# Scaled float16 halves for queries, outputs, experts and router, and shifts and norms moved to GpSimd, in a gated cross-attention and expert layer

## The reference, cut to what matters

```
x = x + tanh(g_xattn) * (softmax(LN(x) Wq (ctx Wk)^T / 8) (ctx Wv) Wo + bo)   # 16 heads of 64
x = x + tanh(g_ffn)   * sum over the 2 best of 8 experts of p_e (LN(x) We^T + be)
```

## Time and profile before

| | |
|---|---|
| runs | 1012.39, 1012.43, 1013.25 us |
| span of the profiled execution | 1009.9 us (its own total time isn't given apart from the runs; the span is 2.5 us below their median) |
| busy PE, DVE, ACT, POOL | 979.5, 821.2, 797.1, 622.4 us |
| chain that ended last | PE 79%, DVE 6%, issue 5%, ACT 4%, POOL 3% |
| DMA engines, transposes and all | 84.7% of 16 engines' span |
| granted clock of PE | full in all slices of the page but the first (0.9) |

### The profile page before, as it was taken

How to read it: one execution, slowest core, us unless ns; L and a number is a source line. 1 busy time by engine, 2 the same in 40 slices (tenths; PEclk the granted TensorE clock), 3 DMA queues, 4 the chain that set the end, 5 groups by cost and what they waited for, 6 DMA issues and landing times.

```text
span 1009.9 us, 27181 instructions
## 1 busy us (share of the span) xinstructions
PE 979.5 (97%) x10656; PEld 770.1 (76%) x10656; DVE 821.2 (81%) x1518; ACT 797.1 (79%) x1404; POOL 622.4 (62%) x371
## 2 busy tenths in 40 slices
PE   7798899999999999999999999999999999999998
PEld 5476777887777877778777787778777787777786
DVE  6577788888888878887888978888788887888768
ACT  5999999777997689886897779977799768987510
POOL 5897777555666557655675746755566655765500
PEclk9899999999999999999999999999999999999999
DMA  4999999787998699995998869977799868998610
GB/s 145 195 205 187 160 182 185 140 128 128 195 166 147 112 161 179 169 151 99 180 169 158 141 115 187 177 138 130 130 190 170 146 110 160 161 154 153 117 35 21
DMA packets 550062, 150.86 MB, mean 149 GB/s; under 512 B 537752, under 2 KB 547376, under 8 KB 549936
## 3 DMA queue, kind: packets, MB, share of 16 engines
q1 hardware_dynamic: 549936, 149.13, 84.7%
HBM read 11.70 MB, written 4.19 MB: 16 GB/s over the span
## 4 chain that ended last, share of the span: by engine, by line
PE 79%; DVE 6%; issue 5%; ACT 4%; POOL 3%; DMA 2%; SPq 0%; ACTq 0%; POOLq 0%; DVEq 0%
PE MB L1076 37%; PE ST L1212 17%; PE PV L1234 16%; PE MB L1088 4%; DVE nmax L873 3%; ACT pf L708 2%; DMA pt_s<-p_s 2%; POOL p_s L552 2%; PE ST L1076 1%; DVE acc L836 1%; PE ST L1243 1%; ACT p_s L718 1%; PE MB L1161 1%; DVE v_s L865 1%; POOL ex_s L590 1%
## 5 line engine op out<-in xcount | busy, mean ns | idle before, releaser
L552 POOL TENSOR_TENSOR p_s<-pf,p_s 128x1024 f16<-128x1024 f32 x254 | 544.3, 2148 | 312.6 <-ACT p_s L718 267.8
L873 DVE TENSOR_REDUCE nmax<-ST 128x2 f32<-128x1024 f32 x256 | 308.4, 1218 | 45.9 <-PE ST L1212 43.0
L708 ACT ACTIVATE pf<-ST,shifts 128x512 f32<-128x512 f32 x512 | 323.8, 688 | 7.6 <-POOL p_s L552 3.7
L718 ACT ACTIVATE p_s<-pf 128x1024 f16<-128x1024 f32 x254 | 267.7, 1060 | 4.2 <-DMA pt_s<-p_s 1.4
L1234 PEld LDWEIGHTS PV<-v_s,pt_s 128*128 128x128 f16 x6096 | 202.2, 98 | 76.7 <-issue 70.4
L1234 PE MATMUL PV<-v_s,pt_s 128*128 128x65 f16 x6096 | 228.8, 194 | 6.4 <-DMA pt_s<-p_s 5.2
L1076 PE MATMUL MB<-ex_s,x2t_s 128*128 128x512 f32 x708 | 189.0, 403 | 0.0
L1076 PEld LDWEIGHTS MB<-ex_s,x2t_s 128*128 128x128 f32 x708 | 126.8, 188 | 24.9
L699 ACT ACTIVATE shifts<-nmax 128x2 f32<-128x2 f32 x256 | 52.8, 206 | 115.8 <-DVE nmax L873 115.3
L836 DVE SCALAR_TENSOR_TENSOR acc<-MB,m,acc 128x256 f32<-128x256 f32 x236 | 113.9, 483 | 29.6 <-PE MB L1076 22.6
L1212 PE MATMUL ST<-KH,QH 64*128 64x512 f32 x512 | 123.0, 476 | 11.4 <-ACT pf L708 8.5
(11 more groups left out here) (141 smaller groups left out, 1047.4 us busy)
## 6 DMA issues: line engine op xcount, KB each, us to landing
pt_s<-p_s SPq DMA_TRANSPOSE x508, 3.4
xin<-x SPq DMA_DIRECT2D x7, 512.0 KB, 4.4
out<-acc SPq DMA_DIRECT2D x7, 512.0 KB, 3.7
kvin<-kv_t SPq DMA_DIRECT2D x8, 256.0 KB, 3.8
acc<-expert_t SPq DMA_DIRECT2D x6, 256.0 KB, 3.5
pf<-wq SPq DMA_DIRECT2D x1, 768.0 KB, 7.2
xin<-x SPq DMA_DIRECT2D x2, 256.0 KB, 2.8
pt_s<-wk SPq DMA_DIRECT2D x1, 512.0 KB, 5.8
```

What stands on the lines that cost most here:

```text
L552: pool.tensor_tensor(p_s[:, slot, 1, :, :], pf[:, u % 2, :, :], p_s[:, slot, 0, :, :], ALU.subtract).then_inc(p_lo, 1)
L708: last = act.activation(pf[:, u % 2, i, :], ST[u % 2][:, i, :], ACT.Exp, bias=shifts[:, u % 2, i:i + 1], scale=SCALE)
L718: act.activation(p_s[:, it.ring(p, u, P_SLOTS), 0, :, :], pf[:, u % 2, :, :], ACT.Copy).then_inc(p_hi, 1)
L873: dve.tensor_reduce(nmax[:, t % 2, :], ST[t % 2][:, :, :], AX.X, ALU.max, negate=True)\
```

## The change

Queries (wq_s, xt_s), output projection (wo_s, ot_s), experts (ex_s, x2t_s) and router (gt_s) are held as float16 high and low parts instead of fp32r; the matmuls on keys, values and scores stay as they are. So that float16 holds them, the weights are divided by a scale taken from their largest absolute value (a maximum over each partition on DVE, summed over the partitions by a small matmul, then five small DVE instructions), and the activations are scaled by 1024 in the norm. The scales go back in where the results are read out. For wq this is done in the prologue (`query_scale`), for the late weights in rows 2 to 8 of the first batch (`late_maximum`, `late_scales`, `gate_parts`); POOL multiplies each late block by its scale in rows 7 to 18, ahead of ACT's copy and POOL's subtraction, which before were in rows 3 to 17. The score scale 1/8 now lies in the query, so that the shift is an addition alone.

The shifts and the applied norms go from ACT to POOL. In POOL's table each row begins with the shift of unit n and goes on with the low part of unit n - 1 instead of n.

```diff
+W_RANGE = 2.0 ** 14
+X_SCALE = 2.0 ** 10
...
 POOL_ORDER = (
-    "low", "low", "low", "low", "low", "low", "low", "low power2", "low", "low residual", "low", "low", "low hold1",
-    "low hold2", "low hold3", "low", "low", "low", "low", "low", "low", "low", "low", "low context power1", "low",
-    "low", "low", "low", "low", "low", "low", "low",
+    "shift low", "shift low", "shift low", "shift low", "shift low", "shift low", "shift low", "shift low",
+    "shift low", "shift power2 norm2 low", "shift low residual", "shift low", "shift low", "shift low",
+    "shift hold1 low", "shift hold2 low", "shift hold3 low", "shift low", "shift low", "shift low", "shift low",
+    "shift low", "shift low", "shift low", "shift low", "shift low power1 norm1", "shift low context", "shift low",
+    "shift low", "shift low", "shift low", "shift low",
 )
 
-VALUES_BACK, SHIFT_BACK, EXP_BACK, COPY_BACK = 6, 0, 0, 0
+VALUES_BACK, LOW_BACK, EXP_BACK, COPY_BACK = 6, 1, 0, 0
...
-NEXT_JOBS = [("xt", 0), ("xt", 1), ("q", 0), ("k", 0), ("bound",), ("q", 1), ("k", 1)]
+NEXT_JOBS = [("xt", 0), ("xt", 1), ("q", 0), ("bound",), ("k", 0), ("q", 1), ("k", 1)]
...
-        wq_s = sb("wq_s", [P, 2, LC, INNER], F32R)
+        wq_s = sb("wq_s", [P, 2, LC, INNER], F16)
         wk_s = sb("wk_s", [P, 2, INNER], F32R)
         wv_s = sb("wv_s", [P, 2, INNER], F32R)
-        wo_s = sb("wo_s", [P, 2, PAIRS, DIM], F32R)
-        ex_s = sb("ex_s", [P, 2, LC, EXPERTS * DIM], F32R)
-        gt_s = sb("gt_s", [P, LC, 2, EXPERTS], F32R)
+        wo_s = sb("wo_s", [P, 2, PAIRS, DIM], F16)
+        ex_s = sb("ex_s", [P, 2, LC, EXPERTS * DIM], F16)
+        gt_s = sb("gt_s", [P, LC, 2, EXPERTS], F16)
...
+                if it.kind == FIRST and n == 0:
+                    sp.dma_start(stage_o[:, :, :], wo.rearrange("(c p) n -> p c n", p=P)).then_inc(wo_in, 16)
+                    sp.dma_start(stage_e[:, :, :], expert_t.rearrange("(c p) n -> p c n", p=P)).then_inc(ex_in, 16)
...
+            def normed(src, n, shift_done, done):
+
+                pool.wait_ge(shift_done, n)
+                for t in range(TT):
+                    last = pool.tensor_scalar(xn[:, t, :], src[:, t, :], rstd[:, t:t + 1], shift[:, t:t + 1],
+                                              ALU.mult, ALU.add)
+                last.then_inc(done, 1)
+
+            def first_norm(it):
+                pool.wait_ge(job_free, it.start(JOBS) + BANKS if it.kind == FIRST else
+                             it.done(JOBS, ("logits",)) + BANKS)
+                normed(xin, it.b + 2, ln1_shift, ln1_done)
+
+            def second_norm(it):
+                pool.wait_ge(job_free, it.start(JOBS) + BANKS)
+                normed(acc, it.b, ln2_shift, ln2_done)
+
+            def shift_of(b, p, u):
+
+                pool.wait_ge(max_done, unit_count(b, p, u))
+                pool.tensor_scalar(shifts[:, u % 2, :], nmax[:, u % 2, :], 1.0, P_SHIFT,
+                                   ALU.mult, ALU.add).then_inc(shift_ready, 1)
...
+                if it.kind == FIRST and 0 <= n - LATE_AT < LATE:
+                    h = n - LATE_AT
+                    if h == 0:
+                        pool.wait_ge(late_scale, 1)
+                    raw, of = late[h][0], late[h][3]
+                    pool.tensor_scalar(raw, raw, late_mul[:, of:of + 1], 1.0, ALU.mult, ALU.mult)\
+                        .then_inc(late_scaled, 1)
+                if it.kind == FIRST and 0 <= n - LATE_AT - LATE_LO < LATE:
+                    h = n - LATE_AT - LATE_LO
                     pool.wait_ge(late_hi, h + 1)
-                    pool.tensor_tensor(late[h][2], late_raw(h), late[h][1].bitcast(F32), ALU.subtract)\
-                        .then_inc(late_lo, 1)
-
-            run(row)
+                    pool.tensor_tensor(late[h][2], late[h][0], late[h][1], ALU.subtract).then_inc(late_lo, 1)
...
+                    act.wait_ge(wq_scale, 3)
+                    act.activation(wq_s[:, 0, :, early], stage_q[:, :, early], ACT.Copy, scale=q_mul[:, 0:1])\
+                       .then_inc(w_hi, 1)
+                    act.wait_ge(wv_in, 16)
+                    act.activation(wv_s[:, 0, :], stage_v, ACT.Copy).then_inc(w_hi, 1)
...
-            def shift_of(b, p, u):
-
-                act.wait_ge(max_done, unit_count(b, p, u))
-                act.activation(shifts[:, u % 2, :], nmax[:, u % 2, :], ACT.Identity, bias=P_SHIFT, scale=SCALE)\
-                   .then_inc(shift_ready, 1)
...
-                                          bias=shifts[:, u % 2, i:i + 1], scale=SCALE)
+                                          bias=shifts[:, u % 2, i:i + 1], scale=1.0)
...
-            def normed(src, n, shift_done, done):
-
-                act.wait_ge(shift_done, n)
-                for t in range(TT):
-                    last = act.activation(xn[:, t, :], src[:, t, :], ACT.Identity, bias=shift[:, t:t + 1],
-                                          scale=rstd[:, t:t + 1])
-                last.then_inc(done, 1)
...
+            def query_scale():
+
+                for n, (cols, landed) in enumerate(((early, wq_in), (rest, wq_rest_in))):
+                    dve.wait_ge(landed, 16)
+                    last = dve.tensor_reduce(wq_max[:, n:n + 1], stage_q[:, :, cols], AX.XY, ALU.max,
+                                             apply_absolute_value=True)
+                last.then_inc(wq_largest, 1)
+                dve.wait_ge(wq_summed, 1)
+                dve.tensor_reduce(q_back[:, :], sums_q, AX.X, ALU.max).then_inc(wq_scale, 1)
+                dve.wait_ge(wq_scale, 1)
+                dve.tensor_scalar(q_div[:, :], q_back[:, :], 1.0 / W_RANGE, 1e-30, ALU.mult, ALU.max)\
+                   .then_inc(wq_scale, 1)
+                dve.wait_ge(wq_scale, 2)
+                dve.tensor_scalar(q_back[:, :], q_div[:, :], SCALE / X_SCALE, None, ALU.mult)
+                dve.reciprocal(q_mul[:, :], q_div[:, :]).then_inc(wq_scale, 1)
...
+                if name == ("bound",):
+                    dve.wait_ge(wv_in, 16)
+                    dve.tensor_reduce(wv_max[:, :], stage_v, AX.X, ALU.max, apply_absolute_value=True)
+                    bound(0)
...
+            def rest_of_queries():
+                dve.wait_ge(w_hi, 4)
+                dve.scalar_tensor_tensor(wq_s[:, 1, :, rest], stage_q[:, :, rest], q_mul[:, 0:1],
+                                         wq_s[:, 0, :, rest], ALU.mult, ALU.subtract).then_inc(wq_rest_lo, 1)
...
+                if kind == FIRST and n == 1:
+                    rest_of_queries()
                 if kind == FIRST and n == 2:
                     constants()
+                if kind == FIRST and 0 <= n - LATE_MAX < 3:
+                    late_maximum(n - LATE_MAX)
+                if kind == FIRST and n == LATE_SUM:
+                    late_scales()
+                if kind == FIRST and n == LATE_AT + 1:
+                    gate_parts()
...
+                    pe.wait_ge(wq_largest, 1)
+                    summed(sums_q, wq_max[:, :], wq_summed)
```

More of the change, by code:

```diff
@@ L818, in take @@
                 elif kind == "router":
-                    last = dve.tensor_copy(logit_parts, m[0:2 * EXPERTS, :])
+                    last = dve.tensor_scalar(logit_parts, m[0:2 * EXPERTS, :], g_back[0:2 * EXPERTS, 0:1], None, ALU.mult)
                 elif kind == "gates":
@@ L1237, in values, with summed @@
                 last.then_inc(pv_ready, 1)
+            def summed(dst, largest, done):
+                pe.matmul(dst, ones[:, :].broadcast_to([P, P]), largest, start=True, stop=True).then_inc(done, 1)
             def keep_busy(n):
```

304 lines of the change are left out of this document (171 added, 133 removed).

## The result

The changed kernel takes 1070.18 us (median of four runs, 1068.18 to 1075.41) against 1012.41 for the kernel before on the same chip: a ratio of 1.058 (95% interval 1.0551 to 1.0608). I had forecast 1031, with a range of 1004 to 1048. It is slower, as forecast, but by 58 us and not by 19. The profiled execution took 1068.53 us, its span is 1066.7.

The account below looks back on a forecast made before the run. PE was taken to pace the middle batches, POOL, ACT and the transposes the first. 1009.9 + 26.3 + 10 + 17 - 35 = 1028.2 us, with 2.5 us from span to median 1031; range 1004 to 1048.

Parts of the forecast that it names:

- scalars in the chains, later batches: PE's waits for POOL after shifts and norms move there: Chain A 10 us plus Chain B 17 us.
- What float16 saves on PE: PE's changed jobs: 4.6 us saved a batch with the router, 35 us in all, nothing in the first batch.
- Rival 4: Float16 saves nothing by itself on PE, only the weight loads: 23 us less saved, 1054 us; chance 0.05.
- What leaves ACT: 256 shifts and the norms leave ACT: hidden in the middle batches, where PE doesn't wait for ACT; costed at nothing.
- What POOL's new instructions cost: On POOL: 0.40 us for 256 elements (norm), 0.70 for 512 (scaling), 0.20 a shift, 0.25 with its wait.
- Rival 3: POOL's scalars cost like two-tile work: 1055 us, or 1045 with 60% of that; chance 0.15.
- Chain A: POOL, rows 9 to 13: a later shift 11 makes the scores of unit 13 wait 1.4 us; seven batches, 10 us.
- Chain B: POOL, rows 25 to 27: the context's low part comes late and k0 waits 2.85 us; six batches, 17 us.
- Prologue: Ahead of the first scores: q0 2.8 us later, 3.6 us more between q0 and k0; +6.4 us.
- First batch: Maxima and scales on DVE +7.9 us; shifts, scalings and later subtractions on POOL in rows 8 to 20 +12 us.
- Rivals 1 and 2: 1: stalls hidden, 1004 us, chance 0.13; 2: first batch takes up its new work, only the prologue stays, 1011 us, 0.12.

Follow-up runs that it names:

- e4: The changed kernel with shifts and norms back on ACT and both engines' orders as before; float16, scales and prologue as changed: 1025.2 us, ratio 1.0123.
- e9_together: e4 with the edits of e6_bound and e7_const, and the gate's low parts on DVE at row 11 instead of 8: 1009.91 us, ratio 0.9971.
- e14_less_scalar: e9_together with one tile of four normalised in the second norm, leaving out three of its four ACT operations: 1007.04 us, ratio 0.9941.
- e2_residual: The changed kernel with `residual` and the load of x moved to row 13, from rows 10 and 9: 1070.88 us, ratio 1.0571.
- e1_context: The changed kernel with the context's low part directly behind row 25's shift on POOL, ahead of low 24, power and norm: 1035.69 us, ratio 1.022.
- e5_busy14: The changed kernel with 14 identity products on PE ahead of k0's wait for the context: 1061.58 us, ratio 1.0482.
- e6_bound: e4 with `bound` behind the first scores, maxima of wv and context ahead of q0's low part, rest of wq rounded while ACT waits: 1019.85 us.
- e7_const: e4 with constant scales for wo, experts and gate, their maxima left out: 1017.45 us, ratio 1.0051.
- e11_scales: e9_together with the scales of wo, experts and gate computed instead of constant: 1014.48 us, ratio 1.002.
- e8: The kernel before, float32r without scales, with the changed kernel's ACT and POOL tables, so shifts and norms on POOL: 1068.55 us, ratio 1.0553.

## Why the prediction was right or wrong

The direction was right, and so were the two places where PE waits for POOL. The size was wrong by 38.5 us of the span (1028.2 against 1066.7), in four terms. The largest is a step that failed: all that float16 saves inside PE's jobs was booked as time of the batch. The next is what the moved scalars cost PE: the clock behind k0's wait, a third stall, and k0's wait in the first batch stood at nothing in my sum.

| step | forecast | measured | off by |
|---|---|---|---|
| float16 on PE | -35 | -16.9 (e4: middle batches 13.8, last 2.3, rest 0.8) | 18.1 |
| scalars in the chains, later batches | +27 | +38.6 (changed less e4: middle batches 36.4, last 0.7, rest 1.5) | 11.6 |
| prologue | +6.4 | +9.3 | 2.9 |
| first batch | +20 | +25.8 | 5.8 |

**What float16 saves on PE**: the step that failed most, in its last sentence. The prices held: an expert job takes 1.46 us, 512 columns come every 216 ns, and inside the jobs 4.3 of the forecast 4.6 us a batch are there. Wrong was to book them whole as time of the batch. The earlier trace rows has PE idle for 0.23 us of 47.60; I read that as PE setting the pace alone, but it doesn't say that the others could follow a faster PE. Of the 4.3 us e4 and e9_together keep 2.4. That some 1.0 us comes back as waits for exponentials is shown; what it is that holds them isn't. It isn't ACT's load alone (e14_less_scalar); what else paces rows 0 to 14 stays open. Rival 4, nothing saved by float16 but the weight loads, is refuted: the matmuls follow each other in 216 ns instead of 233.

**What leaves ACT is costed at nothing**: right as far as the runs show. None isolates it; the nearest, e14_less_scalar, takes 1.55 us a batch from ACT and gains 0.2.

**What POOL's new instructions cost**: the scaling 693 ns (700 forecast) and the shift 197 (200) as forecast, the norm 555 instead of 400, 0.6 us a norm of four. Rival 3, scalars as dear as two-tile work, is wrong for the scalings, and the norms' error, two of them in a middle batch, is worth 1.2 us a batch at most.

**Chain A** (1.4 us forecast): in the changed kernel PE's jobs fall back by 2.0 us against the kernel before between x2t0 and the scores of 14, 0.6 more than forecast, which is the norm's error. But 1.26 of it is already lost at the scores of 12, a wait that my chain passed over, and 0.75 at those of 13. e2_residual shows that `residual`, a third of my chain, could leave it without a gain. That the sum came out near was in part luck.

**Chain B** (2.85): the wait is 3.20, and the fall-back 3.2. Right, and e1_context confirms the order as its cause. Missing was what comes behind the wait, the halved clock, 1.5 us for each 3.4 us of it: some 9 us in all (e5_busy14). Missing too was a third stall, at the scores of unit 24, which wait for exp 22 and its shift: 0.8 us a batch, that none of my chains covers.

**Prologue**: its steps are in the trace, from the sum of maxima at 11.2 to q0's low part; q0 starts 2.4 us later than before (2.8 forecast). What was missing is again the halved clock, which the kernel before doesn't have there. It stands for 3.4 us from 13.3 on, and q0's six matmuls take 2.74 us instead of some 1.46; it stands again from 20.1 on, and k0 takes 1.63 instead of 0.95 and the first scores 1.69 instead of 1.00. These differences add up to 2.7 us, about the 2.9 that were missing. e6_bound gives some 4 of the 9.3 back by the place of `bound`, of its maxima and of the rest of `wq`.

**First batch**: I had +7.9 on DVE, and e7_const shows 6.1 by the maxima; the gate's low parts, that DVE waits for, weren't in my sum at all (5 us, e11_scales). +12 on POOL was right in kind, though no run isolates its size: in rows 11 to 18 of the changed kernel POOL works without a gap, 4.29 us a row.

```profile
91.75 0.19 POOL L573 TENSOR_SCALAR shifts<-nmax 128x2 f32<-128x2 f32 x1
92.02 2.13 POOL L582 TENSOR_TENSOR p_s<-pf,p_s 128x1024 f16<-128x1024 f32 x1
94.13 0.70 POOL L635 TENSOR_SCALAR stage_e<-stage_e,late_mul 128x512 f32<-128x512 f32 x1
94.79 1.16 POOL L640 TENSOR_TENSOR ex_s<-stage_e,ex_s 128x512 f16<-128x512 f32 x1
96.03 0.19 POOL L573 TENSOR_SCALAR shifts<-nmax 128x2 f32<-128x2 f32 x1
```

And k0's first wait, 8.0 us, is in this batch: my chain B was costed for six middle batches, not for the one where it is worst (without it, in e4, rows 27 to 28 lose 0.6 us, with it 9.4). Up to row 27 the changed kernel's first batch is 16.7 us behind, 3 less than the whole forecast: that 25.8 looks near to 20 hides a sum that was too large and a wait that wasn't in it. The clock plays in here too. The table ahead of the prediction has the one slice below full speed as the first; it is the page's second, and the lower level stands there for 6.8 us from 42.4 on, in the first batch (0.92 in the earlier trace rows). In the changed kernel's first batch it stands for 35 us in all; what that costs there no run separates. Rivals 1 and 2 are refuted: the stalls are not hidden, and of its new work the first batch takes up little.

**The parts don't add.** The scalars alone cost 56.2 us (e8), float16 and scales alone 12.3 (e4), together 57.8 and not 68.5. In the first batch e8 has +20.2, e4 +18.2 and the changed kernel +25.8: the waits for late weights and for shifts lie partly beside each other.

## What to carry to other kernels

Before a small operation on the critical loop is moved off the engine that consumes its result, look at what it will queue behind. Shifts of 0.2 us, and norms with them, moved to an engine whose other work comes in pieces of 2 us, cost 45 to 56 us in the order first written and 13 in the mended one, and no run shows a gain from the engine that they left; shifts and norms weren't priced apart. A saving on an engine that is busy 99% is time of the kernel only as far as its neighbours have room to follow; and price a new wait with the clock that follows it. Where work must be moved, look first at what stands in the same in-order queue ahead of the one value that the bound engine needs: here one row's order was worth 34.5 us.
